# Mixture stage with its loops written out: row transposes moved ahead of the gate and up matmuls, one register load per slot

## What is computed

```python
logits = jnp.einsum('bsh,eh->bse', x, router_w)
idx = jnp.argmax(logits, axis=-1).reshape(-1)
for e in range(E):                       # 8 experts, 512 wide
    g = bitlinear(xf, wg[e])
    u = bitlinear(xf, wu[e])
    y = bitlinear(jnp.square(jax.nn.relu(g)) * u, wd[e])
    out = out + jnp.where((idx == e)[:, None], y, 0.0)
```

## Time and profile before

| what | value |
| --- | --- |
| median of 3 runs | 1772.18 us (1770.33 to 1776.66) |
| the profiled execution | 1772.23 us |
| its span, first to last instruction | 1770.4 us |
| instructions | 24758 |
| TensorE busy | 1454.6 us, 82% |
| VectorE busy | 1258.1 us, 71% |
| ScalarE busy | 970.7 us, 55% |
| mean granted TensorE clock | 0.913 |
| the mixture stage | about 561 to 679 us |

### The profile page before, as it was taken

How to read it: one execution, slowest core, us unless ns; L and a number is a source line. 1 busy time by engine, 2 the same in 40 slices (tenths; PEclk the granted TensorE clock), 3 DMA queues, 4 the chain that set the end, 5 groups by cost and what they waited for, 6 DMA issues and landing times. The chain is left out here.

```text
span 1770.4 us, 24758 instructions
## 1 busy us (share of the span) xinstructions
PE 1454.6 (82%) x8465; PEld 839.6 (47%) x8536; DVE 1258.1 (71%) x1520; ACT 970.7 (55%) x1440; POOL 438.6 (25%) x343
## 2 busy tenths in 40 slices
PE   4999988999551774878999999999826599999996
PEld 3554534555240333323555555555403366666663
DVE  4888856655582676859999999999448686655551
ACT  5878723344171555414777777767612376665551
POOL 0122210000313004304555555555752000000000
PEclk9999998999755996878999999999958699999998
DMA  6788650000083226420423233331177396666640
GB/s 220 244 276 290 204 205 1 0 0 0 1 354 111 72 90 186 111 79 11 97 74 95 76 92 79 90 81 28 36 213 226 115 327 219 219 220 219 220 142 28
DMA packets 145938, 236.92 MB, mean 134 GB/s; under 512 B 11320, under 2 KB 61496, under 8 KB 144704
## 3 DMA queue, kind: packets, MB, share of 16 engines
q1 hardware_dynamic: 140352, 210.65, 38.5%
q0 software_dynamic: 5504, 25.20, 3.9%
HBM read 169.74 MB, written 59.59 MB: 130 GB/s over the span
## 5 line engine op out<-in xcount | busy, mean ns | idle before, releaser
L1632 ACT ACTIVATE t_e<-t_psE 128x512 f32<-128x512 f32 x512 | 304.6, 597 | 133.6 <-PE t_psE L1725 124.9
L1670 DVE TENSOR_REDUCE t_nmax<-t_psM 128x1 f32<-128x1024 f32 x256 | 301.5, 1212 | 15.7 <-PE t_psM L1706 15.6
L1591 POOL TENSOR_TENSOR t_low<-t_e 128x1024 bf16<-128x1024 f32 x128 | 250.0, 1955 | 196.4 <-ACT t_e L1632 186.7
L1736 PE MATMUL t_psO<-t_e,vst 128*96 128x512 bf16 x512 | 200.6, 392 | 2.4 <-POOL t_low L1591 2.4
L1725 PE MATMUL t_psE<-qst,kst 99*128 99x512 bf16 x512 | 195.2, 382 | 0.1
L1736 PE MATMUL t_psO<-t_low,vst 128*96 128x512 bf16 x512 | 193.1, 377 | 0.0
L1678 DVE TENSOR_TENSOR t_low<-t_e 128x1024 bf16<-128x1024 f32 x128 | 177.9, 1390 | 18.3 <-ACT t_e L1632 17.8
L1706 PE MATMUL t_psM<-kst,qst 96*128 96x512 bf16 x512 | 164.0, 404 | 28.0 <-DVE t_nmax L1670 22.7
L2218 PE MATMUL e_psG<-xeT,e_w1p 128*128 (+1 forms) x1536 | 172.8, 276 | 9.4 <-DVE e_hT L2162 4.8
L2218 PEld LDWEIGHTS e_psG<-xeT,e_w1p 128*128 128x128 bf16 x1536 | 151.7, 99 | 30.9 <-issue 5.9
L2233 PE MATMUL e_psO<-e_w2p,e_hT 128*128 128x512 bf16 x752 | 164.9, 379 | 0.8
(11 more groups left out here) (229 smaller groups left out, 2309.3 us busy)
## 6 DMA issues: line engine op xcount, KB each, us to landing
piece<-in_L_ffn_w SPq DMA_DIRECT2D x32, 1024.0 KB, 13.5
xres<-in_L_ffn_w SPq DMA_DIRECT2D x32, 1024.0 KB, 15.2
wT<-ternary POOLq DMA_DIRECT2D x8, 1536.0 KB, 21.4
kst<-keys SPq DMA_DIRECT2D x96, 128.0 KB, 4.2
mixed<-t_ost SPq DMA_DIRECT2D x64, 192.0 KB
c_rows<-in_ctx SPq DMA_DIRECT2D x8, 1024.0 KB, 10.3
xres<-in_L_ffn_wg SPq DMA_DIRECT2D x8, 1024.0 KB, 7.6
xres<-in_L_ffn_wu SPq DMA_DIRECT2D x8, 1024.0 KB, 7.1
```

What stands on the lines that cost most here:

```text
L1591: nc.gpsimd.tensor_tensor(low[:, slot(h, u), :, :], e32[:, slot(h, u), :, :], upper(h, u), ALU.subtract).then_inc(lo_pool, 1)
L1632: nc.scalar.activation(e32[:, slot(h, u), i, :], psE[:, i, :], ACT.Exp, scale=SC).then_inc(expd, 1)
L1670: nc.vector.tensor_reduce(nmax[:, h // G % 2, h % G, u:u + 1], banks_of(place_of_max(b, m)).rearrange("p a t -> p (a t)"), AX_X, ALU.max, ...
L1736: last = nc.tensor.matmul(psO[0:VW, h % 2, :], vst[:, g, 2 * u + i, :].rearrange("p (w h) -> p h w", h=G)[:, h % G, :], part[:, i, :], sta ...
```

## The change

The loops of all four engines at work in the stage are written out (each slot's number is then a constant). On TensorE x_transposes(j+3) comes before gate_and_up(j+2); on ScalarE x_copy(j+3) comes before q_casts(j+1). The expert's number is read once, in gate_and_up, kept in a register and used again by down. The conditions of every wait stay as they are.

```diff
@@ sync
-                with sp.Fori(0, (NS - 4) // 4) as i:
-                    for k in range(4):
-                        load(4 * i + k + 4, k)
-                        store(4 * i + k, k % 2)
-                for j in range((NS - 4) // 4 * 4, NS):
+                for j in range(NS):
                     if j + 4 < NS:
                         load(j + 4, j % 4)
                     store(j, j % 2)
@@ scalar
                 def step(j, par, left):
                     h_copy(j, par)
+                    if left >= 3:
+                        x_copy(j + 3, 1 - par)
                     if left >= 1:
                         q_casts(j + 1, 1 - par)
                     if left >= 2:
                         squares(j + 2, par)
-                    if left >= 3:
-                        x_copy(j + 3, 1 - par)
...
-                with act.Fori(0, MAIN // 2) as i:
-                    step(2 * i, 0, 3)
-                    step(2 * i + 1, 1, 3)
-                for j in range(MAIN, NS):
+                for j in range(NS):
                     step(j, j % 2, NS - 1 - j)
@@ vector
-                with dve.Fori(0, (NS - 4) // 4) as i:
-                    for k in range(4):
-                        step(4 * i + k, k % 2, 2, True, k)
-                for j in range((NS - 4) // 4 * 4, NS):
+                for j in range(NS):
                     step(j, j % 2, NS - 1 - j, j + 4 < NS, j % 4)
@@ tensor
+                experts = {}
+
                 def weights_of(j):
-                    e = nc.tensor.value_load(expert_of[0:1, bass.ds(j, 1)], min_val=0, max_val=E - 1)
+                    e = experts[j]
                     return lambda m, k: wT[:, bass.ds(e, 1), m, :, k, :].rearrange("p o r d -> p (o r) d")
 
                 def gate_and_up(j, par):
+                    experts[j] = nc.tensor.value_load(expert_of[0:1, bass.ds(j, 1)], min_val=0, max_val=E - 1)
                     w = weights_of(j)
...
                 def step(j, par, left, slot3):
                     h_transposes(j, par)
+                    if left >= 3:
+                        x_transposes(j + 3, slot3)
                     if left >= 2:
                         gate_and_up(j + 2, par)
-                    if left >= 3:
-                        x_transposes(j + 3, slot3)
                     down(j, par)
+                    del experts[j]
...
-                with pe.Fori(0, (NS - 4) // 4) as i:
-                    for k in range(4):
-                        step(4 * i + k, k % 2, 3, (k + 3) % 4)
-                for j in range((NS - 4) // 4 * 4, NS):
+                for j in range(NS):
                     step(j, j % 2, NS - 1 - j, (j + 3) % 4)
```

More of the change, by code:

```diff
@@ L991, in mixture_phase @@
         out_v = mixture_dram.rearrange("(n p) d -> n p d", p=P)
-        MAIN = (NS - 3) // 2 * 2
-        assert NS - 3 == MAIN
         with nc.Block() as block:
```

## The result

The changed kernel takes **1793.83 us** (median of 7 runs) beside 1772.48 us of the kernel before (7 runs): ratio 1.0112, interval 1.0092 to 1.0133, 21 us slower in the medians. Forecast were 1781.6 us and a range up to 1790. The direction was right, the size too small by more than half.

What follows compares the result with a forecast made beforehand. It took a VectorE-ScalarE dependence ring to bound the stage, replaced after the change by a two-slot chain of 10.0 us through the row loads. Stage +8.4 and code +1 gave +9.4 on 1772.18: 1781.6 us, range 1776 to 1790.

Steps and rivals of the forecast that it cites:

- Writing out gains up to 4.6 us: Loops as constants: 16 slot intervals fall from 4.57 to 4.28 us, gaining 4.6 us if nothing else is late.
- One register load fewer is worth nothing: TensorE before down: gate and up finish 0.5 us early, so the load is off the path; 0, bounds -5.3 and 0.
- Row transposes now queue behind a load that stands behind a store: TensorE: load(s+5) waits behind store(s), so transposes and then gate and up wait for DMA; stage +8.4 us.
- The ring's sum of 10.0 us: Chain from m_ys through load, transposes, gate and up, relu, product to next m_ys: 10.0 us for two slots; chance 0.78.
- gate and up: 1.91: Term of the two-slot chain: TensorE's gate and up matmuls with their first weight load take 1.91 us.
- TensorE now pauses about 1 us before the x transposes: TensorE was to idle about 1 us per slot waiting for rows, 18 times, and 0.5 us behind the transposes.
- 70% busy: TensorE's forecast share of busy time in the stage, 3.5/5.0, little less than the 75% at clock 1.00.
- the clock falls: Rival: TensorE's pauses drop the granted clock to 0.50, 15 us more over nine pairs, 1797 us; chance 0.09.
- ScalarE's order costs nothing: x_copy(j+3) ahead of the cast, about 0.6 us, fits in ScalarE's 1.54 us idle while its transposes are done.
- Code +1 us: Instruction fetches for twelve to sixteen more slots make some loads land 0.5 us later; +1 us, bounds 0 and 5.
- Product 2 moves by 0 ± 0.4: Start of product 2: four added transposes against a shorter written-out relu-to-product; taken as 0, bounds ±0.4 us.
- the ring between VectorE and ScalarE: Product, m_q, cast, relu, square, with no TensorE work: 4.28 us a slot written out, 4.57 in the loop.

Runs made afterwards that it cites:

- e1: All loops written out, but the kernel before's order on TensorE and ScalarE and both register loads kept; 1766.95 us, ratio 0.9970 to the kernel before.
- e2: e1 with the expert's number read once per slot and kept in a register; 1767.67 us, ratio 0.9977 to the kernel before.
- e7: Changed kernel with the register load for gate and up issued ahead of the row transposes; 1786.88 us, ratio 1.0053 to the kernel before.
- e9: e8 with the register load of slot j+3 issued ahead of down(j); 1754.88 us, ratio 0.9885 to the kernel before.
- e8: Written out, e3's earlier loads, gate_and_up first in TensorE's step, ScalarE's relu ahead of the cast, square behind it; 1764.41 us, ratio 0.9942 to the kernel before.
- e3: Changed kernel with SyncE issuing load(j+5) instead of load(j+4) ahead of store(j); 1768.03 us, ratio 0.9980 to the kernel before.
- e6: Changed kernel with ScalarE's old order (x_copy after the squares), only TensorE's order new; 1788.51 us, ratio 1.0069 to the kernel before.
- e5: Kernel before, loops and both register loads kept, with the new TensorE and ScalarE order alone; 1806.71 us, ratio 1.0174 to the kernel before.
- e4: Changed kernel with ten unused identity transposes per slot ahead of the row transposes; 1786.36 us, ratio 1.0081 to the kernel before.

## Why the prediction came out as it did

- *Writing out gains up to 4.6 us*: right, 4.6 in the stage (e1).
- *One register load fewer is worth nothing*: right (e2). Estimated from the Trainium skill's floor for a register load (DMA: Bandwidth & Descriptors, Latency and other measured facts) it would have been 13.8 us if it were on the path; it isn't. e7 and e9 show that the load that stays can be: there its place, not its number, counts. What a load left open in these traces is less than the skill's floor or about as much: 0.58 us before down in the kernel before, 0.47 behind the transposes after the change, 0.28 in e8.
- *Row transposes now queue behind a load that stands behind a store*: right, and the cause (e3).
- *The ring's sum of 10.0 us*: seven of eight terms within 0.05 us in the changed kernel. The step that failed is the term "gate and up: 1.91", taken from rows at the full clock. It measured 3.41 on average, nine times.
- Behind it lies the sentence "TensorE now pauses about 1 us before the x transposes". It divided a pair's wait evenly over two slots. The prediction's own terms said otherwise: h transposes are done some 3.5 us after product s+2 (the cast ends at 3.1, they take 0.4) and the rows land at 5.83, so TensorE has nothing to do for 2.3 us at a stretch. That is what came, 2.3 us in one piece ahead of every second slot, and the second slot followed at its own 4.28. From 70% busy on average I judged the clock safe. The rival *the clock falls* had the mechanism, and its 1797 us was 3 us off; 0.09 was too small a chance, for a mechanism that then ran nine times of nine. The Trainium skill's page on it (TensorE: Matmul & The Clock Gate, HAM oscillation — how this bites in real kernels) describes matmul groups that start slow after each DMA wait; this trace agrees, though the DMA waits of its example are longer than those here: 3.40 and 3.59 us behind pauses of 2.3.
- *ScalarE's order costs nothing*: by its own wait, yes; through the clock it goes with a loss of 8 us by the ratios, 6 us in the stage (e6 against the change, two chips, intervals that just miss each other).
- *Code +1 us*: instruction packets rose from 4 (560 to 680 us) to 10 (560 to 700 us), but the landing's median stayed 2.2 and the ring without gate and up is 11.50 - 3.41 = 8.09, as forecast. The one landing of 3.0 us, beside an instruction packet, was of a load that TensorE did not wait for. No cost is seen.
- *Product 2 moves by 0 ± 0.4*: it came 1.56 us sooner. Gate and up of step 0 took 1.90 us, where the trace of before has 3.1; in e1, with no transposes ahead of them, they took 1.90 too, and so they did in e5's loops, while in e6, written out, they took 2.79. So the difference is the clock's in one execution or another, not the edit's; the 1.6 us are luck of the two executions compared.

## What to carry over

Before moving work forward on an in-order engine, look up when its input is issued, not only when it was ready in the old place: the row transposes had looked free because gate and up covered a transfer that is issued late, behind a store. When a chain closes over two slots, lay out both of them; the average hides whether TensorE pauses twice for 1 us or once for 2.3, and in these traces the clock mostly fell behind the long ones. The order that lost 20 us cost nothing once the load went out one slot sooner (e3), but gained nothing either, because the ring between VectorE and ScalarE set the pace. The gain of 19 us (e9) came when the relu left that ring and the register load no longer stood in front of gate and up; there gate and up stand ahead of the row transposes again, and of the changed order only x_copy's place is kept.

## What was not expected of the hardware

In the changed kernel gate and up ran at a granted clock of 0.50 to 0.58 on average (3.2 to 3.6 us instead of 1.9) behind every one of nine DMA waits of 2.2 to 2.6 us, though TensorE was busy 52 of 72 us over the stage. The traces of the changed kernel and of e4 to e7 hold 54 such waits of the row transposes from step 2 on. Behind 27 of the 30 that lasted 2.1 us or more gate and up took 2.7 to 3.6 us; behind the other three (2.18 in e4, 2.44 and 2.25 in e7) they took 1.9. Behind the 24 of 1.8 us or less they took 1.9, but for one (1.59 in e6, then 3.55). So the length of the pause goes with the fall of the clock, but doesn't decide it alone; what else does is not shown by any run here.

What the register load costs was also a surprise: nothing where TensorE has time (e2), 0.28 us of idle time a slot in e8, and 8.5 us in all over the stage when e9 moved it (83.4 to 74.9).
